# Keys' side of a last attention layer loaded ahead into dead rows, and its fill reordered

## The chip, the cores and the metric

One NeuronCore of a Trainium2 chip runs the whole kernel. Its engines are TensorE (PE, with its weight load PEld), VectorE (DVE), ScalarE (ACT), GpSimd (POOL) and SyncE (SP), which here does nothing but wait and issue DMAs. Each engine runs its own instructions in order and waits on semaphores. The metric is the time of one execution on the device in microseconds.

## The reference, cut to what matters

The rows `x` are 8 sequences of 256 rows of 256 features, and the context `ctx` has the same shape. Two layers follow each other:

```
layer 0: x = LN(x)                                      # pre-norm, then
         y = LN(y + mha(y, y))     ; y = LN(y + mha(y, ctx))   # 16 heads of 16, masked
         y = LN(y + relu(y@w1)@w2)
         x = x + tanh(g0) * y
         x = x + tanh(g0f) * moe_top2(LN(x))            # 8 experts, 256 -> 1024 -> 256
layer 1: q = rope(LN(x) @ Wq) ; k = rope(ctx @ Wk) ; v = ctx @ Wv
         x = x + tanh(g1) * (softmax(q k^T / 8) v @ Wo) # no context depends on x
         x = x + tanh(g1f) * moe_top1(LN(x))
```

Keys and values of layer 1 come from the context alone, queries from the rows that layer 0 leaves.

## The kernel before, in words

The program is three stages with a barrier between them, all matrices in f32, scores in split bf16 parts.

**Attention stage** (`attention_pipeline`). 16 units (8 sequences x 2 attentions) move through a pipeline of beats, one unit per beat, 16 heads per beat; `b` is the beat. In the beat `b`, head 14, TensorE turns the context of unit `b + 4` (`turn_context`, units 8 to 15 only) into a PSUM bank, and ScalarE copies it to the one SBUF tile `cT` (`bring_context`); keys and values of that unit are projected from `cT` in the next beat. SP's program is written out per beat: `stack(b + 2)`, `spread_parts(b + 3, 0)`, `spread_parts(b + 3, 1)`, `max_to_queries(b + 1)`, loads. Two PSUM banks are shared by all small tasks in turn, in the order of `TASKS`.

**Expert stage** (`feed_forward_and_experts`). First 8 sequences pass a dense feed-forward; VectorE forms the new rows (`rows`, `new_rows`), the router picks two experts (`top_experts`, `destinations`), and POOL scatters the normed rows `Y` to DRAM by expert (`scatter`). Then `SLOTS` = 39 slots of 128 rows run, 12 of them (`EARLY_SLOTS`) before all sequences are sorted. Per slot: SP loads its rows from DRAM (`load`, 128 KB, into the one tile `xs`), TensorE turns them (`turn_slot`), VectorE copies the expert's first matrix to one of two places (`expert_matrix`, line 2644), TensorE multiplies up (`up_slot`, line 2350), ScalarE applies relu, TensorE multiplies down (`down_slot`, line 2362), VectorE adds the bias (`slot_rows`), SP stores (`store`). TensorE's order in the loop is up s, turn s + 1, down s - 1. SP's is `load(s + 1)`, `store(s - 1)`. After the last scatter nothing reads `Y` any more.

**Last stage** (`rotary_and_experts`). SP loads weights, tables and contexts (`load_rotary`) into the space where the experts' matrices come later. A fill precedes the beats: for sequences 0 to 2, POOL gathers each row's two expert outputs with indirect DMAs (`gather`, four calls, line 1624), VectorE adds them to `X` (`sum_rows`, line 1847) and takes moments (`input_moments`), POOL computes the inverse roots in 14 tiny steps (`input_roots`, lines 134 to 141), VectorE norms (`input_norm`, line 151, into `Y`), TensorE turns (`turn_rows`) and projects queries (line 1185); the contexts are turned (`turn_context`, line 1176), copied to `cT`, and projected to keys (line 1185) and values (line 1208). VectorE rotates keys and queries (`turned`, lines 1771 and 1773). Each is then split into three bf16 parts by POOL and ScalarE in turn (`parts`: lines 1600, 1605, 1610 on POOL, with two copies on ScalarE between; `split` on ScalarE), and SP writes them to DRAM and reads them back as stacks (`spread_parts`, `stack`). Scores, their maxima, and the beats follow. In a beat `b`, head 14, `turn_context(b + 4)` and `bring_context(b + 4)` run here too. `first_expert` is POOL's load of expert 0 over the space of the contexts.

The order of POOL's work in the fill is written out by hand:

```python
gather(0); gather(1); input_roots(0); parts(0, 1); parts(0, 0); input_roots(1)
gather(2); parts(1, 1); parts(1, 0); input_roots(2); gather(3); parts(2, 1); gather(4); parts(2, 0)
```

Of the kernel before, what the change touches and what calls it, by code (L numbers as in the profile page):

```python
# [14 lines left out]
P = 128  # L15
# [322 lines left out]
def attention_pipeline(nc, tag, c, mem, X, Y, cross, masks, fills, keys_out, loads, ff):  # L338
# [7 lines left out]
    with ExitStack() as ctx:  # L346
# [47 lines left out]
        filled0 = sem("filled0")  # L394
# [9 lines left out]
        def _(sp):  # L404
# [40 lines left out]
            sp.wait_ge(filled0, 16 * (len(fills) + 1))  # L445

# [155 lines left out]
        def _(act):  # L602
# [264 lines left out]
FILL = ("c", 0), ("k", 0), ("v", 0), ("x", 0), ("q", 0), ("c", 1), ("k", 1), ("v", 1), ("x", 1), ("q", 1), ("c", 2), ("k", 2), ("v", 2)  # L867
LAST_FILL = {2: (("x", 2),), 5: (("q", 2),), 9: (("m", 0),), 12: (("x", 3),), 14: (("c", 3),)}


def rotary_tasks(b, h):
# [4 lines left out]
    units = [(k, QUADS * b + d if k == "o" else b + d) for k, d in TASKS.get(h, ()) + ROUTE_TASKS.get(h, ())]  # L876
# [15 lines left out]
def rotary_memory(nc, ctx, tag, w_in, keys, key_off, tables, ctx_in, stack_rows):  # L892
# [11 lines left out]
    w = {"wq": by_chunk(part("W2", 1, 0)), "wk": by_chunk(part("W2", 1, 1)), "wv": by_chunk(part("W2", 1, 2)), "wo": sb("wo", [P, NC, D])}  # L904
# [3 lines left out]
    return {"w": w, "w_in": w_in, "keys": keys, "key_off": key_off, "tables_in": tables, "ctx_in": ctx_in, "stack_rows": stack_rows,  # L908
            "W1": W1, "W2": W2, "w1s": w1s,
            "C": [by_chunk(part(("W1", "W2")[m // 4], 0, m % 4)) for m in range(B)],  # L910
            "tables": {k: by_chunk(part("W1", 1, i)) for i, k in enumerate(tables)},
            "fq": part("W2", 1, 3), "fk": part("W1", 2, 0), "rq": part("W1", 2, 1), "rk": part("W1", 2, 2), "tq": part("W1", 2, 3),
            "tk": part("W2", 2, 0), "cT": by_chunk(part("W2", 2, 1)),
# [13 lines left out]
def load_context_of(sp, mem, n):  # L927

    sp.dma_start(mem["C"][n], mem["ctx_in"][n].rearrange("(u p) d -> p u d", p=P)).then_inc(mem["c_in"][n], 16)


def load_rotary(sp, mem):

    w, w_in = mem["w"], mem["w_in"]

    def matrix(k, done):
        sp.dma_start(w[k][:, :, :], w_in[k].rearrange("(c p) n -> p c n", p=P)).then_inc(done, 16)
# [10 lines left out]
    load_context_of(sp, mem, 0)  # L948
    matrix("wk", mem["k_in"])
    columns("bk", mem["k_in"])  # L950
    table("cosk", mem["k_in"])
    table("sink", mem["k_in"])
    matrix("wv", mem["v_in"])
    row("bv", mem["v_in"])
    sp.dma_start(mem["mcu"][:, :], mem["keys"].rearrange("b (u p) -> p (b u)", p=P), allow_slow_non_contiguous=True).then_inc(mem["v_in"], 16)
    matrix("wq", mem["q_in"])
# [3 lines left out]
    load_context_of(sp, mem, 1)  # L960
    load_context_of(sp, mem, 2)
# [13 lines left out]
def rotary_and_experts(nc, tag, c, mem, X, Y, L, gate, yd, dest, weight, gate_f, ids_dram, rows_dram, out, w1_in, w2_in, b1_in, b2_in, wg_in, bg_in):  # L975
# [3 lines left out]
    W1, W2, w1s = mem["W1"], mem["W2"], mem["w1s"]  # L979
# [7 lines left out]
    with ExitStack() as ctx:  # L987
# [5 lines left out]
        xT, cT, aT, yT = sb("xT", [P, NC, SEQ]), mem["cT"], sb("aT", [P, NC, SEQ]), sb("yT", [P, NC, SEQ])  # L993
# [163 lines left out]
        def _(pe):  # L1157
            ident, identb = c["ident"], c["identb"]

            def turn_rows(m):  # L1160
# [3 lines left out]
                for cc in range(NC):  # L1164
                    for u in range(NU):
                        ins = nc.tensor.transpose(dst[:, cc * SEQ + u * P:cc * SEQ + (u + 1) * P],
                                                  here(Y, m)[:, u, cc * P:(cc + 1) * P], ident[:, :])
                ins.then_inc(filled("x", m), 1)

            def turn_context(m):  # L1170
                pe.wait_ge(mem["c_in"][m], 16)
                pe.wait_ge(*free("c", m))
                dst = bank_of("c", m)
                for cc in range(NC):
                    for u in range(NU):
                        ins = nc.tensor.transpose(dst[:, cc * SEQ + u * P:cc * SEQ + (u + 1) * P],
                                                  C[m][:, u, cc * P:(cc + 1) * P], ident[:, :])
                ins.then_inc(filled("c", m), 1)
# [10 lines left out]
            def queries(m):  # L1189
                if m == 0:  # L1190
                    pe.wait_ge(mem["q_in"], 16 * 4)
# [3 lines left out]
            def keys(m):  # L1195
                if m == 0:
                    pe.wait_ge(mem["k_in"], 16 * 4)
                pe.wait_ge(*taken("c", m))
                product("k", m, w["wk"], cT)

            def project_values(m):
                if m == 0:
                    pe.wait_ge(mem["v_in"], 16 * 3)
                pe.wait_ge(*free("v", m))
                dst = bank_of("v", m)
                for u in range(NU):
                    for kc in range(NC):
                        ins = nc.tensor.matmul(dst[:, u * D:(u + 1) * D], cT[:, kc, u * P:(u + 1) * P], w["wv"][:, kc, :],  # L1208
# [144 lines left out]

            turn_context(0)
            keys(0)
            project_values(0)
            turn_rows(0)
            queries(0)
            turn_context(1)
            keys(1)  # L1360
            project_values(1)
            turn_rows(1)
            queries(1)
            turn_context(2)
# [4 lines left out]
            for h in range(H):  # L1369
# [9 lines left out]
                if h == 14:  # L1379
                    turn_context(3)  # L1380
            early = lambda n: 0 <= n < EARLY_ONES - 1
            for b in range(0, M):
                for h in range(H):
# [18 lines left out]
                    if h == 14 and has(b + 4):  # L1402
                        turn_context(b + 4)
# [48 lines left out]
        def _(act):  # L1452
# [5 lines left out]

            def bring_context(m):
                if m >= 1:  # L1460
                    act.wait_ge(*full("v", m - 1))
                act.wait_ge(*full("c", m))
                nc.scalar.activation(flat(cT[:, :, :]), bank_of("c", m)[:, :], ACT.Copy).then_inc(emptied("c", m), 1)
# [68 lines left out]
            bring_context(0)  # L1532
            bring_rows(0)
            split(0, 1)
            bring_context(1)
            split(0, 0)
            bring_rows(1)
            split(1, 1)
            bring_context(2)
# [5 lines left out]
            bring_context(3)  # L1545
            early = lambda n: 0 <= n < EARLY_ONES - 1
            for b in range(0, M):
                for h in range(H):
# [14 lines left out]
                    if h == 14 and has(b + 4):  # L1563
                        bring_context(b + 4)
# [31 lines left out]
        def _(pool):  # L1596
# [71 lines left out]
            def first_expert():  # L1668
                pool.wait_ge(*full("c", M - 1))
# [91 lines left out]
        def _(dve):  # L1761
# [92 lines left out]
            def input_norm(n):  # L1854
                dve.wait_ge(rooted0, n + 1)
                normal_rows(nc, here(X, n), here(Y, n), t0).then_inc(x_normed, 1)
# [118 lines left out]
            dve.wait_ge(mem["v_in"], 16 * 3)  # L1975
            nc.vector.tensor_copy(mcf[:, :], mem["mcu"][:, :]).then_inc(kept_in, 1)
            value_rows(0)
            sum_rows(1)
            input_moments(1)
            dve.wait_ge(mem["q_in"], 16 * 4)  # L1980
            queries(0)
            turned_keys(1)
            input_norm(1)
            value_rows(1)
# [170 lines left out]

def feed_forward_memory(nc, ctx, a):
# [646 lines left out]
```

## Time and profile before

| what | value |
|---|---|
| median of 3 runs | 1408.83 us (1404.21 to 1412.75) |
| profiled execution, its own time | 1403.39 us |
| span of its instructions | 1401.5 us |
| TensorE busy | 1219.7 us (87%), mean granted clock 0.945 |
| VectorE busy | 769.8 us (55%) |
| ScalarE busy | 560.6 us (40%) |
| POOL busy | 500.7 us (36%) |
| DMA, mean over the span | 111 GB/s |
| expert stage, first slot to last | 583.8 to 896.8 us |
| last stage, fill | 900.7 to about 1000.1 us |

The span runs from the first to the last instruction of the core; the execution's own time is 1.9 us more. Busy shares are averages over stages with different limits, so a stage has to be read by itself. The granted clock is the share of TensorE's full clock (2.4 GHz) that it was given; 0.50 is 1.2 GHz.

### The profile page before, as it was taken

How to read it: one execution, taken by the hardware profiler on the slowest of the kernel's cores; microseconds unless marked ns; L12 is line 12 of the kernel's file. 1: busy time of each engine (PE TensorE's matmuls, PEld its weight loads, DVE VectorE, ACT ScalarE, POOL GpSimd, SP SyncE). 2: the span in 40 equal slices, each digit the busy share in tenths (PEclk: the TensorE clock that was granted, in tenths of full speed). 3: DMA queues.
4: the chain of work that ended last, by engine and by line, in shares of the span. 5: the costliest groups of instructions: out<-in, count | busy, mean ns of one | idle time of the engine just before them, and what ended most of it. 6: DMA issues, size and time to landing. Idle time of an engine off the chain costs nothing. (4 is left out here: it accounts for less than half of the span.)

```text
span 1401.5 us, 27155 instructions
## 1 busy us (share of the span) xinstructions
PE 1219.7 (87%) x8465; PEld 973.2 (69%) x8520; DVE 769.8 (55%) x2825; ACT 560.6 (40%) x1350; POOL 500.7 (36%) x895
## 2 busy tenths in 40 slices
PE   4699999999998999898999999656687878689996
PEld 3466667777755888788888898533455655589995
DVE  4687777777783487842412121147788876533331
ACT  2265565666665332233333333111354546133331
POOL 3334354454524244420000000256765543433331
PEclk9799999999999999999999999865799999799999
DMA  4776785756520950111111111356364597511110
GB/s 118 163 169 189 198 205 156 162 155 152 145 63 11 356 195 31 42 58 35 36 34 36 34 38 32 85 131 149 99 146 105 85 279 230 180 33 43 41 34 6
DMA packets 126580, 156.16 MB, mean 111 GB/s; under 512 B 19531, under 2 KB 112089, under 8 KB 121564
## 3 DMA queue, kind: packets, MB, share of 16 engines
q1 hardware_dynamic: 116648, 127.14, 35.2%
q0 software_dynamic: 9792, 27.30, 6.3%
q8 instruction: 71, 1.16, 0.4%
q14 instruction: 69, 0.57, 0.2%
HBM read 104.43 MB, written 52.32 MB: 112 GB/s over the span
## 5 line engine op out<-in xcount | busy, mean ns | idle before, releaser
L764 DVE CUSTOM_DVE_ANT_0 att_masked_scores<-att_S,Bm 128x256 bf16<-128x256 f32 x512 | 192.5, 419 | 69.4 <-PE att_S L508 55.4
L645 ACT ACTIVATE att_PT<-att_T 128x512 f32<-128x512 f32 x256 | 151.4, 595 | 93.6 <-PE att_T L527 84.8
L2437 ACT ACTIVATE moe_hT<-moe_H,moe_b 128x128 f32<-128x128 f32 x312 | 89.0, 369 | 194.9 <-PE moe_H L2350 193.6
L2350 PE MATMUL moe_H<-moe_aT,ff_w 128*128 128x128 f32 x1248 | 146.2, 275 | 8.4 <-DVE ff_w L2644 8.4
L2350 PEld LDWEIGHTS moe_H<-moe_aT,ff_w 128*128 128x128 f32 x1248 | 145.1, 192 | 11.7 <-DVE ff_w L2644 9.9
L2362 PE MATMUL moe_Z<-moe_W,moe_hT 128*128 x624 | 142.5, 381 | 0.8 <-DVE moe_z L2651 0.8
L1624 POOL DMA_INDIRECT L_W<-yd,dest x32 | 31.3, 977 | 278.4 <-POOLq L52 269.9
L2362 PEld LDWEIGHTS moe_Z<-moe_W,moe_hT 128*128 128x128 f32 x624 | 115.4, 190 | 15.5 <-issue 1.2
L2651 DVE TENSOR_TENSOR moe_z<-moe_Z,moe_b 128x256 f32<-128x256 f32 x39 | 16.5, 424 | 199.5 <-PE moe_Z L2362 199.5
L508 PE MATMUL att_S<-L_KS,L_QS 96*128 96x256 bf16 x512 | 99.3, 276 | 19.6 <-DMA L_KS<-att_k_dram 14.5
L527 PE MATMUL att_T<-L_QS,L_KS 99*128 99x256 bf16 x512 | 98.7, 273 | 4.8 <-issue 2.3
L1800 DVE TENSOR_REDUCE out_mx<-out_S 128x2 f32<-128x512 f32 x128 | 85.7, 683 | 17.1 <-PE out_S L1218 14.8
L1520 ACT ACTIVATE X<-out_T,L_b 128x128 f32<-128x128 f32 x184 | 52.5, 370 | 98.4 <-PE out_T L1337 97.1
L1337 PEld LDWEIGHTS out_T<-out_xT,L_w1s 128*128 128x128 f32 x736 | 87.5, 196 | 4.7 <-issue 2.1
L1337 PE MATMUL out_T<-out_xT,L_w1s 128*128 128x128 f32 x736 | 88.2, 279 | 2.9 <-issue 1.5
L1486 ACT ACTIVATE L_W<-out_T 128x512 f32<-128x512 f32 x128 | 72.7, 596 | 39.7 <-PE out_T L1236 37.2
L1350 PE MATMUL out_S<-L_W,X 128*128 x368 | 83.5, 380 | 2.1 <-DVE out_ys L1962 2.1
L527 PEld LDWEIGHTS att_T<-L_QS,L_KS 99*128 99x128 bf16 x512 | 50.6, 99 | 38.9 <-issue 1.1
L525 PE MATMUL att_T<-BmT,identb 128*128 128x512 bf16 x201 | 77.0, 383 | 0.4
L1218 PE MATMUL out_S<-L_W 97*128 97x256 bf16 x256 | 54.7, 303 | 25.9 <-DVE out_mx L1800 20.3
L1350 PEld LDWEIGHTS out_S<-L_W,X 128*128 128x128 f32 x368 | 68.1, 190 | 11.5 <-issue 3.2
L508 PEld LDWEIGHTS att_S<-L_KS,L_QS 96*128 96x128 bf16 x512 | 48.0, 98 | 33.6 <-DMA L_KS<-att_k_dram 16.0
(465 smaller groups left out, 2385.5 us busy)
## 6 DMA issues: line engine op xcount, KB each, us to landing
moe_W<-in_L_ffn_W SPq DMA_DIRECT2D x16, 1024.0 KB, 13.7
xd<-zero SPq DMA_DIRECT2D x12, 1280.0 KB
L_W<-in_L_ffn_W POOLq DMA_DIRECT2D x12, 1024.0 KB, 15.3
att_q_dram<-att_pq SPq DMA_DIRECT2D x16, 384.0 KB
att_k_dram<-att_pk SPq DMA_DIRECT2D x16, 384.0 KB
L_QS<-att_q_dram SPq DMA_DIRECT2D x16, 384.0 KB
L_KS<-att_k_dram SPq DMA_DIRECT2D x16, 384.0 KB
moe_xs<-xd SPq DMA_DIRECT2D x39, 128.0 KB
```

The lines of the kernel that those rows point to most:

```text
L508: ins = nc.tensor.matmul(bankS[h % 2][:, u * SEQ:(u + 1) * SEQ], QS[0:ROWS, m % 3, h, u * P:(u + 1) * P], KS[0:ROWS, m % 3, h, :], start=T ...
L525: nc.tensor.matmul(dst[:, :], identb[:, :], masks[m // B][1][:, :], start=True, stop=False)
L527: ins = nc.tensor.matmul(dst[:, u * SEQ:(u + 1) * SEQ], KS[0:ROWS_ALL, m % 3, h, u * P:(u + 1) * P], QS[0:ROWS_ALL, m % 3, h, :], start=Fa ...
L645: nc.scalar.activation(PT[:, h % 8, :], bankT[h % 2][:, :], ACT.Exp).then_inc(exp_done, 1)
L764: ins = nc.vector.tensor_tensor_reduce(masked_scores[:, h % 2, u, :], bankS[h % 2][:, u * SEQ:(u + 1) * SEQ], masks[m // B][0][:, u * SEQ: ...
L1337: ins = nc.tensor.matmul(bankH[half][:, f * P:(f + 1) * P], matrix[:, cc, k * P:(k + 1) * P], xT[:, s % 2, cc * P:(cc + 1) * P], start=(cc ...
L1350: ins = nc.tensor.matmul(bankY[:, 0:D], eT[:, s % 2, f * P:(f + 1) * P], matrix[:, f, :], start=(f == 0), stop=(f == NF - 1))
L1486: nc.scalar.activation(PT[h % 8], bankT[h % 2][:, :], ACT.Exp).then_inc(exp_done, 1)
L1800: nc.vector.tensor_reduce(mx[:, m % 2, :, h:h + 1], bankS[h % 2][:, :].rearrange("p (u k) -> p u k", u=NU), AXX, ALU.max).then_inc(max_don ...
L2350: ins = nc.tensor.matmul(bankH[half][:, f * P:(f + 1) * P], w1s[:, cc, g * P:(g + 1) * P], xT[:, s % 2, cc * P:(cc + 1) * P], start=(cc == ...
L2362: ins = nc.tensor.matmul(bankZ[:, 0:D], eT[:, s % 2, f * P:(f + 1) * P], w2e[:, f, :], start=(f == 0), stop=(f == NF - 1))
L2437: ins = nc.scalar.activation(eT[:, s % 2, g * P:(g + 1) * P], bankH[half][:, f * P:(f + 1) * P], ACT.Relu, bias=b1[:, bass.ds(e * NF + g, 1)])
```

## The change

**Attention stage.** After ScalarE has filled `cT` for units 8 to 15, SP stores it to a DRAM tensor `turned_ctx` (`keep_context`), once per unit, before the spreads of the same beat. ScalarE's `bring_context` waits for the store of the unit before.

**Expert stage.** `turn_router(6)` and its copy on ScalarE move from ahead of slot 0 to behind it, `logits(6)` and `rank(6)` one slot later, `expert_matrix(0)` ahead of `new_rows(6)`, `expert_matrix(2)` ahead of `new_rows(7)`, `top_experts(6)` and `destinations(6)` one slot later. At slot 12, ahead of the load of slot 13's rows, SP issues eight loads (`load_entry`) into `Y`: `wk`, `wv`, `wq`, the two tables of the keys, and the turned contexts 0 to 2.

**Last stage.** No context is turned: keys and values multiply from the loaded turned contexts, the five others come from `turned_ctx` through `load_rest`. `cT` and the `c` tasks of the shared banks are gone. `input_norm` writes to two tiles `xn` in turn instead of `Y`. `load_rotary` keeps only the biases, the mask, the two tables of the queries and the constant rows. The orders of all engines in the fill are written anew. `first_expert` waits for the values of sequence 7 where it waited for its turned context.

```diff
+            def keep_context(m):
+                sp.wait_ge(*taken("c", m))
+                sp.dma_start(turned_ctx[m - B], flat(cT[:, :, :])).then_inc(ctx_kept, 16)
             for b in BEATS:
                 if has(b + 2):
                     stack(b + 2)
+                if has(b + 3) and cross(b + 3):
+                    keep_context(b + 3)
...
                 act.wait_ge(*full("c", m))
+                if m > B:
+                    act.wait_ge(ctx_kept, 16 * (m - B))
...
+ENTRY_CONTEXTS = 3
+ENTRY = "wk", "wv", "wq", "cosk", "sink"
+def load_entry(sp, Y, entry, entered):
+    contexts, places = entry_places(Y)
+    for k in ENTRY:
+        sp.dma_start(places[k], entry[k].rearrange("(c p) n -> p c n", p=P)).then_inc(entered, 16)
+    for n in range(ENTRY_CONTEXTS):
+        sp.dma_start(contexts[n], entry["contexts"][n].rearrange("p (c t) -> p c t", c=NC)).then_inc(entered, 16)
...
+                if s == EARLY_SLOTS:
+                    sp.wait_ge(r_turned, B)
+                    load_entry(sp, Y, entry, entered)
                 if s + 1 < SLOTS:
                     load(s + 1)
                 if s >= 1:
                     store(s - 1)
...
+                if n == B - 1:
+                    expert_matrix(0)
                 new_rows(n - 1)
...
-            expert_matrix(0)
             rows(B - 1)
+            expert_matrix(1)
             for s in range(SLOTS):
...
+                if s == 0:
+                    expert_matrix(2)
+                    new_rows(B - 1)
+                if s >= 2 and s + 1 < SLOTS:
                     expert_matrix(s + 1)
...
             gather(0)
+            parts(0, 1)
+            input_roots(0)
             gather(1)
-            input_roots(0)
-            parts(0, 1)
             parts(0, 0)
             input_roots(1)
+            parts(1, 1)
             gather(2)
-            parts(1, 1)
             parts(1, 0)
             input_roots(2)
...
             nc.vector.memset(V[:, :, :, :], 1.0).then_inc(ready0, 1)
+            dve.wait_ge(mem["k_in"], 16)
+            turned_keys(0)
+            dve.wait_ge(mem["v_in"], 16 * 2)
+            nc.vector.tensor_copy(mcf[:, :], mem["mcu"][:, :]).then_inc(kept_in, 1)
+            value_rows(0)
             sum_rows(0)
             input_moments(0)
-            dve.wait_ge(mem["k_in"], 16 * 4)
-            turned_keys(0)
+            turned_keys(1)
+            value_rows(1)
             input_norm(0)
```

On ScalarE the fill begins `split(0, 1)`, `bring_rows(0)`, `split(0, 0)`, `first_part(1, 1)`, `bring_rows(1)`, `second_part(1, 1)`; on TensorE keys and values of sequences 0 and 1, then their rows and queries, then keys and values of sequence 2.

## Rows read from the trace of the kernel before

**Rows 1.** Windows of the fill and of a later beat; columns stand in the head line.

```profile
core 0: us, PE busy (x) PEld busy (x) DVE busy (x) ACT busy (x) POOL busy (x), PEclk, DMA share, GB/s
900.70:1000.10 99.40, 57.10 (x190) 36.60 (x190) 53.68 (x147) 13.68 (x23) 66.02 (x127) 0.63 0.63 150
...
1040.00:1050.00 10.00, 9.17 (x80) 5.65 (x78) 8.54 (x23) 4.55 (x10) 7.12 (x18) 1.00 0.80 185
```

**Rows 2.** What POOL waited for, 898 to 1004 us: us in total, times, longest.

```profile
POOL out_xve L134 <- DVE out_xmv L118: 8.3, 2, 4.5
POOL L_W L1605 <- ACT L_W L1476: 7.3, 7, 2.9
...
POOL L_W L1600 <- DVE L_W L1773: 2.0, 1, 2.0
```

**Rows 3.** Timeline of POOL in the fill: start, us, then line, operation, idle before.

```profile
900.75 0.99 POOL L1624 DMA_INDIRECT L_W<-yd,dest  x1 [269.85 <-POOLq L52]
902.04 0.97 POOL L1624 DMA_INDIRECT L_W<-yd,dest  x1 [0.30 <-issue]
...
914.37 0.21 POOL L134 TENSOR_SCALAR out_xve<-out_xmv 128x2 f32<-128x2 f32 x1 [3.86 <-DVE out_xmv L118]
...
918.14 1.26 POOL L1600 TENSOR_TENSOR L_W<-L_W 128x512 f32<-128x512 f32 x1
...
941.29 1.28 POOL L1600 TENSOR_TENSOR L_W<-L_W 128x512 f32<-128x512 f32 x1
...
946.31 1.26 POOL L1600 TENSOR_TENSOR L_W<-L_W 128x512 f32<-128x512 f32 x1
```

**Rows 4.** Timeline of VectorE (DVE) in the fill.

```profile
911.34 1.88 DVE L1847 SCALAR_TENSOR_TENSOR X<-L_W,weight,X 128x256 f32<-128x256 f32 x4 [8.44 <-DMA L_W<-yd,dest]
...
918.22 1.65 DVE L151 TENSOR_SCALAR Y<-X,out_xmv,out_xr 128x256 f32<-128x256 f32 x2 [2.39 <-POOL out_xr L141]
...
926.82 0.48 DVE L1773 SCALAR_TENSOR_TENSOR L_W<-out_A,L_bq,L_W 128x256 f32<-128x256 f32 x1
...
1000.28 1.65 DVE L151 TENSOR_SCALAR Y<-X,out_xmv,out_xr 128x256 f32<-128x256 f32 x2 [3.89 <-POOL out_xr L141]
```

**Rows 5.** Timeline of TensorE (PE), last stage.

```profile
921.78 3.75 PE L1185 MATMUL out_A<-out_xT,L_W 128*128 128x256 f32 x8 [0.73 <-ACT out_xT L1457]
...
1016.67 0.60 PE L1176 MATMUL out_B<-ident,L_W 128*128 128x128 f32 x4
```

**Rows 6.** Timeline of TensorE, slots of the expert stage.

```profile
583.77 3.84 PE L2350 MATMUL moe_H<-moe_aT,ff_w 128*128 128x128 f32 x32 [2.43 <-DVE ff_w L2644]
...
590.51 3.84 PE L2350 MATMUL moe_H<-moe_aT,ff_w 128*128 128x128 f32 x32 [1.89 <-DVE ff_w L2644]
...
599.09 3.84 PE L2350 MATMUL moe_H<-moe_aT,ff_w 128*128 128x128 f32 x32 [0.86 <-DVE ff_w L2644]
...
685.48 0.44 PE L2337 MATMUL moe_T<-ident,moe_xs 128*128 128x128 f32 x2 [0.18 <-DMA moe_xs<-xd]
...
690.26 3.84 PE L2350 MATMUL moe_H<-moe_aT,ff_w 128*128 128x128 f32 x32 [0.85 <-DVE ff_w L2644]
```

**Rows 7.** Timeline of SP's DMA issues, slots and fill.

```profile
682.32 0.33 SPq L2237 DMA_DIRECT2D yd<-moe_z  x1
683.40 0.34 SPq L2233 DMA_DIRECT2D moe_xs<-xd  x1
...
974.50 2.64 SPq L929 DMA_DIRECT2D L_W<-in_ctx  x5
```

**Rows 8.** Context loads of the last stage, from issue to landing.

```profile
DMA to landing us min/median/max: 2.9/6.1/7.2
```

**Rows 9.** Windows of 2 us in the fill, columns as in rows 1.

```profile
978.00:980.00 2.00, 1.60 (x6) 0.39 (x6) 2.00 (x6) 0.62 (x1) 1.21 (x2) 0.50 0.95 184
982.00:984.00 2.00, 0.00 (x0) 0.00 (x0) 0.21 (x1) 0.00 (x0) 1.50 (x9) 0.50 1.11 349
1002.00:1004.00 2.00, 1.34 (x8) 0.63 (x12) 2.00 (x5) 1.70 (x5) 1.16 (x1) 0.60 0.00 0
1004.00:1006.00 2.00, 2.00 (x20) 0.80 (x13) 2.00 (x5) 0.88 (x3) 1.90 (x2) 0.54 0.00 0
```

More of the change, by code:

```diff
@@ L889, in rotary_banks, with rotary_memory @@
     return {task: (i % 2, i // 2) for i, task in enumerate(order)}
-def rotary_memory(nc, ctx, tag, w_in, keys, key_off, tables, ctx_in, stack_rows):
+def rotary_memory(nc, ctx, tag, w_in, keys, key_off, tables, turned_ctx, stack_rows, Y):
     sb = lambda n, s, d=F32: ctx.enter_context(nc.sbuf_tensor(f"{tag}_{n}", s, d))
@@ L903, in rotary_memory @@
     PARTS = 3 * NC * SEQ // 2
-    w = {"wq": by_chunk(part("W2", 1, 0)), "wk": by_chunk(part("W2", 1, 1)), "wv": by_chunk(part("W2", 1, 2)), "wo": sb("wo", [P, NC, D])}
+    contexts, entered = entry_places(Y)
+    w = {"wo": sb("wo", [P, NC, D]), **{k: entered[k] for k in ("wq", "wk", "wv")}}
     w.update({k: sb(k, [P, NC]) for k in ("bq", "bk")})
@@ L907, in rotary_memory @@
     stacks = lambda a: a.rearrange("p (e h t) -> p e h t", e=3, h=H)
-    return {"w": w, "w_in": w_in, "keys": keys, "key_off": key_off, "tables_in": tables, "ctx_in": ctx_in, "stack_rows": stack_rows,
+    return {"w": w, "w_in": w_in, "keys": keys, "key_off": key_off, "tables_in": tables, "ctx_in": turned_ctx, "stack_rows": stack_rows,
             "W1": W1, "W2": W2, "w1s": w1s,
-            "C": [by_chunk(part(("W1", "W2")[m // 4], 0, m % 4)) for m in range(B)],
-            "tables": {k: by_chunk(part("W1", 1, i)) for i, k in enumerate(tables)},
+            "C": contexts + [by_chunk(part(("W1", "W2")[m // 4], 0, m % 4)) for m in range(ENTRY_CONTEXTS, B)],
+            "tables": {"cosk": entered["cosk"], "sink": entered["sink"], **{k: by_chunk(part("W1", 1, i)) for i, k in enumerate(tables)}},
+            "xn": [by_chunk(part("W2", 1, i)) for i in range(2)],
             "fq": part("W2", 1, 3), "fk": part("W1", 2, 0), "rq": part("W1", 2, 1), "rk": part("W1", 2, 2), "tq": part("W1", 2, 3),
-            "tk": part("W2", 2, 0), "cT": by_chunk(part("W2", 2, 1)),
+            "tk": part("W2", 2, 0),
             "pq": three(half["W2", 2][:, 2 * NC * SEQ:2 * NC * SEQ + PARTS]), "pk": three(half["W2", 3][:, 0:PARTS]),
@@ L968, in load_rest @@
     w, w_in = mem["w"], mem["w_in"]
-    for n in range(3, B):
+    for n in range(ENTRY_CONTEXTS, B):
         load_context_of(sp, mem, n)
@@ L1166, in turn_rows @@
                         ins = nc.tensor.transpose(dst[:, cc * SEQ + u * P:cc * SEQ + (u + 1) * P],
-                                                  here(Y, m)[:, u, cc * P:(cc + 1) * P], ident[:, :])
+                                                  xn[m % 2][:, u, cc * P:(cc + 1) * P], ident[:, :])
                 ins.then_inc(filled("x", m), 1)
[L1170 to L1178, printed above, removed]
             def product(kind, m, wt, src):
@@ L1352, in down_slot @@
                 ins.then_inc(y_ready, 1)
[L1354 to L1364, printed above, removed]
+            for m in range(2):
+                keys(m)
+                project_values(m)
+            for m in range(2):
+                turn_rows(m)
+                queries(m)
             keys(2)
@@ L1530, in split @@
                 second_part(m, side)
-            bring_context(0)
+            split(0, 1)
             bring_rows(0)
-            split(0, 1)
-            bring_context(1)
             split(0, 0)
+            first_part(1, 1)
             bring_rows(1)
-            split(1, 1)
-            bring_context(2)
+            second_part(1, 1)
             split(1, 0)
@@ L1668, in first_expert @@
             def first_expert():
-                pool.wait_ge(*full("c", M - 1))
+                pool.wait_ge(*full("v", M - 1))
                 load_expert(pool, 0)
@@ L1855, in input_norm @@
                 dve.wait_ge(rooted0, n + 1)
-                normal_rows(nc, here(X, n), here(Y, n), t0).then_inc(x_normed, 1)
+                if n >= 2:
+                    dve.wait_ge(*full("x", n - 2))
+                normal_rows(nc, here(X, n), xn[n % 2], t0).then_inc(x_normed, 1)
                 dve.wait_ge(x_normed, n + 1)
@@ L2385, in _ @@
                 if s == 0:
+                    turn_router(B - 2)
+                if s == 1:
                     logits(B - 2)
-                if s == 1:
+                if s == 2:
                     rank(B - 2)
-                if s == 2:
                     turn_router(B - 1)
@@ L2719, in weights_of @@
                     "gain": a[f"L0_xattn_{norm}_g"], "shift": a[f"L0_xattn_{norm}_b"]}
+        wkv, bkv = a["L1_xattn_Wkv"], a["L1_xattn_bkv"]
+        w = {**{k: a["c_L1_" + k] for k in ("wq", "bq", "wk", "bk")}, "wv": wkv[:, D:2 * D], "bv": bkv[D:2 * D],
+             "wo": a["L1_xattn_Wo"], "bo": a["L1_xattn_bo"]}
         with ExitStack() as f:
```

93 lines of the change are left out of this document (32 added, 61 removed).

## The prediction

> **What bounds the kernel now.** I read the windows first, since the change touches four places with different limits. In the expert stage (about 580 to 900 us) TensorE is the bound. The fill of the last stage, 900.7 to 1000.1 us, is the weak stretch: TensorE is busy 57.1 of 99.4 us at a mean clock of 0.63, POOL 66.0 us, and no engine is full, while a later beat has TensorE 9.17 and VectorE 8.54 of 10 us at full clock [rows 1]. Of POOL's gaps there some are waits for others: 8.3 us in two waits for moments, 2.0 us for VectorE's turned keys, and one wait of 2.9 us for ScalarE where 0.74 is usual, in all 8.3 + 2.0 + 2.1 = 12.4 us [rows 2]. The timelines show POOL paces the rest: it runs roots, gathers and parts back to back, and VectorE waits 3.89 us for the roots of the fifth sequence at the fill's end [rows 3, 4]. So the fill is worth at most these 12.4 us to a reordering that leaves POOL's work as it is.
>
> **Attention stage: contexts kept.** Added: eight stores of 256 KB, one a beat, issued on SP between `stack(b + 2)` and the spreads, and a wait on ScalarE before `bring_context` for the store of one beat earlier. `cT` was filled a beat before SP asks, so SP does not wait; the store lands in microseconds [rows 8] and the beat is over 20 us. Behind it in SP's order stand the two spreads, which wait for parts of their own. Cost 0; were that cover gone, one 256 KB transfer (at most 2.9 us, rows 8) would delay one stack.
>
> **Expert stage, turn from rows to slots.** `expert_matrix(0)` moves ahead of `new_rows(6)`, and `turn_router(6)` behind the first slot. Before, TensorE waited 2.43, 1.89 and 0.86 us for the copies of slots 0, 1 and 2 [rows 6]. Slot 0 now starts some 2.6 us sooner, but copy 1 still stands behind the same VectorE work (`new_rows(6)`, `destinations(5)`, `rows(7)`; only the copy changed places), so up-projection 1 still starts at 590.5: the first gain turns into a longer wait there. Copy 2 now precedes `new_rows(7)`, so 0.86 us is gained. Against it, the two short waits have become one of about 4.3 us. After a wait of that size the clock fell: in 1002 to 1006 us it was 0.60 and 0.54, which is 2 x 0.40 + 2 x 0.46 = 1.7 us of full-clock work lost [rows 9]. I take the loss: -0.9 + 1.7 = **+0.8** (bounds -0.9 and +0.8).
>
> **Expert stage, entry load.** Eight DMAs of 256 KB (three weights, two tables, three contexts, 2.10 MB) enter SP's queue at slot 12, ahead of the load of slot 13's rows. SP is free there after the store at 682.3, and issued load 13 at 683.4; TensorE turned it at 685.48 after waiting 0.18 us for that very DMA [rows 6, 7]. So this load has no slack. Each issue takes SP about 0.52 us (five contexts in 2.64, rows 7), eight take 4.1. If only the issue counts, load 13 leaves at 687.5 and lands at 689.4, 3.9 us late; TensorE waited 0.85 us soon after for the copy behind `pack_destinations` [rows 6], which is absorbed: **+3.1**, the lower bound. If the bytes also go first, with the rows themselves they are 2.23 MB. The best rate in a stretch of context loads is 349 GB/s, the worst 184 [rows 9]; a lone 256 KB needs 2.9 us, of which 0.75 is bytes at 349, so 2.1 is fixed [rows 8]. Landing is then 682.7 + 2.1 + 6.4 = 691.2, 5.7 us late, 4.8 after the absorbed wait; TensorE stands idle nearly 6 us, and I add 2.5 us for the clock, between one fall (1.7) and two (3.4). **+7.3**. At 184 GB/s: 682.7 + 2.1 + 12.1 = 696.9, 10.5 net, with 3.4 for the clock **+13.9**, the upper bound. I take 7.3, since these are contiguous rows as in the faster stretch, while the slow one held small-row stacks.
>
> The trace has large loads and small ones behind them landing late. The Trainium skill ("DMA: Bandwidth & Descriptors", Queues, rings and completion order) says that on each DMA engine descriptors are consumed in ring order. By that rule the 128 KB load waits for all 2.10 MB; without it, the sum would take the lower bound. The same page (Specifications) gives about 358 GB/s from HBM; by that figure, an estimate, the bytes take 6.2 us and the sum changes by 0.2.
>
> **Last stage, fill.** Removed: turning three contexts in the fill (four with the last half), their copies, 2 MB of loads at the entry. POOL's pieces keep their lengths: a gather 4 x 1.27 - 0.3 = 4.8, roots 3.8 (914.37 to 918.14), parts 5.05 (941.29 to 946.31) [rows 3]. New order, from POOL's first at 900.75:
> gather(0) to 905.6. Keys(0) need no load but the bias: TensorE 3.75 at half clock [rows 5], VectorE 1.6, ready at about 905.6. Parts(0,1) to 910.7. Gather(0) lands 2.9 later, 908.5 (before, at 911.3 behind the loads, rows 4); sums 1.9 and moments 1.0: 911.4, a wait of **0.7**. Roots(0) to 915.3, gather(1) to 920.1. Parts(0,0) needs queries(0), which before came 9.1 us after the start of the norm (918.22 to 927.30, rows 4), so 924.4: a wait of **4.3**. Then roots(1), parts(1,1) (second part behind `bring_rows(1)`: **0.2**), gather(2), parts(1,0), roots(2), whose moments wait for gather(2) (**0.8**), gather(3), parts(2,1), gather(4), parts(2,0), whose queries wait behind ScalarE's `split(2, 1)` (**0.8**); the rest as before. Waits 6.8 in place of 12.4: **-5.6**. Bounds: if gather(0) lands as late as before, 2.8 less, -2.8; if TensorE is at full clock for queries(0) and the turns, 2.0 us of that wait go, -7.6. What is late next is the roots of sequence 4, still POOL's. The copy of `mcu` is now ahead of the first sums; its DMA is issued third and has until 908.5.
>
> **Last stage, beats.** Five turns of a context leave TensorE (0.60 us each, rows 5) with their ScalarE copies: 3.0 us at most. VectorE is nearly as full as TensorE in a beat [rows 1], so most is hidden: **-1.0** (0 to -3.0). `first_expert` waits for v(7) instead of c(7), which POOL's own `keep_values(7)` has awaited already: 0.
>
> **Sum.** 0 + 0.8 + 7.3 - 5.6 - 1.0 = +1.5 on the profiled execution's own 1403.39 (span 1401.5 and 1.9 around it): 1404.9. The median of the runs is 1408.83, 5.4 above that execution, so **1410.3**. A step of 0.5% is 7 us, about what this kernel's measurement can tell from nothing.
>
> **Rivals.**
> *Only the issue costs.* Slot 13's rows overtake the entry load; the entry load costs 3.1. For it: no row shows this pair of transfers; against: load 13 is the last in the same queue. 0.8 + 3.1 - 5.6 - 1.0 = -2.7: 1406.1.
> *The fill gives more.* TensorE stays warm between the early keys and queries(0), no clock is lost at the slots, and the beats gain all five turns: -0.9 + 3.1 - 7.6 - 3.0 = -8.4, 1400.4. For it: keys and values of two sequences now run in one piece; against: some 4 us of idle follow them, and the clock's mean of 0.63 in the fill [rows 1].
> *Slower: the entry load at the slow rate.* One stall at slot 13 worth 13.9 (above): 0.8 + 13.9 - 5.6 - 1.0 = +8.1, 1416.9. It decides for slower from a stall of 12.8. For it: the stretch at 184 GB/s also held context loads [rows 9]; against: its small rows.
>
> **Chances.** Forecast 0.48 (of it 0.02 below and 0.04 above the 0.5% lines), issue only 0.12, more from the fill 0.22, slow load 0.18, with what resembles it. Faster 0.22 + 0.02 = 0.24, same 0.42 + 0.12 = 0.54, slower 0.18 + 0.04 = 0.22. The two outer cases are 1400.4 and 1416.9; with the runs' own scatter the range is 1400 to 1418. The forecast's own range is 1405 to 1415.
>
> **What would show it.** Right: one TensorE gap of 5 to 7 us before the turn of slot 13, released by the rows' DMA, with half clock behind it; up-projection 1 still released by its copy; POOL's first parts at 905.6 after the stage's start, its wait before parts(0,0) near 4 us, and the roots of sequence 4 some 6 us nearer the stage's start. Wrong: slot 13 on time, a stage start that moved for other reasons, a POOL wait for queries(0) over 8 us, or scores that wait for a stack in the beats.

## The result, and the profile after

The changed kernel takes 1414.61 us (median of 20 runs, 1408.08 to 1421.87), the kernel before 1403.97 (20 runs, 1397.66 to 1412.75). The ratio is 1.0071, 95% interval 1.0058 to 1.0085: slower by 0.7%, some 10 us. The forecast was +1.5 us. It was made on a median of 1408.83 us from three runs, which twenty runs put at 1403.97; so the changed kernel's time lies in the forecast's range (1405 to 1415) by luck: the time before was taken 4.9 us too high, and that hid half of the miss. The difference, which is what matters, is missed by 9 us, and a slowdown above 0.5% had a chance of only 0.22. The profiled execution of the changed kernel has a span of 1414.1 us, against 1401.5.

I cut both spans at the same instructions: the first turn of slot 0, the turns of slots 12 and 14 on TensorE, POOL's first gather in the last stage (gather(0)) and its gather(5) at the end of the fill. The lengths, in us:

| kernel | to slot 0 | slots 0 to 12 | slots 12 to 14 | slot 14 to gather(0) | fill, to gather(5) | rest | span |
|---|---|---|---|---|---|---|---|
| before | 581.0 | 96.8 | 16.1 | 206.8 | 90.1 | 410.6 | 1401.5 |
| changed | 584.4 | 98.2 | 25.4 | 206.0 | 92.0 | 408.1 | 1414.1 |

The largest item is at slots 12 to 14, **+9.2** (25.37 against 16.13). It is one stall and the half clock behind it (0.50 from 694 to 702 us). TensorE's timeline of the changed kernel in the slots, with the two slots of the turn from rows to slots first:

```profile
585.54 3.81 PE L2341 MATMUL moe_H<-moe_aT,ff_w 128*128 128x128 f32 x32 [0.72 <-issue]
...
593.51 5.44 PE L2341 MATMUL moe_H<-moe_aT,ff_w 128*128 128x128 f32 x32 [3.50 <-ACT moe_aT L2420]
...
603.35 3.73 PE L2341 MATMUL moe_H<-moe_aT,ff_w 128*128 128x128 f32 x32
...
697.44 0.69 PE L2328 MATMUL moe_T<-ident,moe_xs 128*128 128x128 f32 x2 [7.35 <-DMA moe_xs<-xd]
697.93 6.26 PE L2353 MATMUL moe_Z<-moe_W,moe_hT 128*128 x16
704.02 3.73 PE L2341 MATMUL moe_H<-moe_aT,ff_w 128*128 128x128 f32 x32
```

Where 0.18 us of waiting stood before the turn of slot 13 [rows 6], 7.35 stand now, and the down-projection behind it lasts 6.26 us where 3.62 to 3.65 is usual. SP's issues of the changed kernel, and its window over the stall:

```profile
687.12 0.33 SPq L2224 DMA_DIRECT2D yd<-moe_z  x1
687.50 0.43 SPq L2137 DMA_DIRECT2D Y<-in_c_L_wk  x1
...
690.05 1.42 SPq L2139 DMA_DIRECT2D Y<-turned_ctx  x3
692.21 0.35 SPq L2220 DMA_DIRECT2D moe_xs<-xd  x1
```

```profile
core 0: us, PE busy (x) PEld busy (x) DVE busy (x) ACT busy (x) POOL busy (x), PEclk, DMA share, GB/s
...
690.00:700.00 10.00, 2.65 (x8) 2.17 (x8) 3.82 (x12) 1.52 (x5) 0.00 (x0) 0.65 0.57 188
```

The rows' load leaves at 692.21 and is awaited until 697.4, 5.2 us, and the granted clock of the window is 0.65.

The fill was to become 5.6 us shorter and is **1.9 longer**. The window of the whole fill, to the norm of sequence 4 [rows 1], and what POOL waited for in it [rows 2]:

```profile
913.95:1015.40 101.45, 51.00 (x174) 31.46 (x173) 56.11 (x148) 11.51 (x19) 66.27 (x128) 0.61 0.53 127
```

```profile
POOL out_xve L134 <- DVE out_xmv L118: 10.3, 2, 6.7
...
POOL L_W L1575 <- ACT L_W L1451: 4.7, 6, 1.0
POOL L_W L1565 <- DVE L_W L1738: 3.8, 2, 3.4
```

POOL is busy as before (66.0, now 66.3). TensorE has 6 us less to do, which buys nothing. The waits of my sum were 12.4 us before, I forecast 6.8, and they are 10.3 + 3.8 + 0.3 = 14.4 (the 0.3 is what the longest wait for ScalarE, 1.0, has above the usual 0.74). POOL's timeline and VectorE's show where [rows 3, 4]:

```profile
913.98 0.98 POOL L1589 DMA_INDIRECT L_W<-yd,dest  x1 [278.75 <-POOLq L52]
...
917.79 0.95 POOL L1589 DMA_INDIRECT L_W<-yd,dest  x1 [0.30 <-issue]
919.14 1.26 POOL L1565 TENSOR_TENSOR L_W<-L_W 128x512 f32<-128x512 f32 x1 [0.41 <-DVE L_W L1738]
...
930.87 0.21 POOL L134 TENSOR_SCALAR out_xve<-out_xmv 128x2 f32<-128x2 f32 x1 [6.68 <-DVE out_xmv L118]
...
942.99 1.43 POOL L1565 TENSOR_TENSOR L_W<-L_W 128x512 f32<-128x512 f32 x1 [3.36 <-DVE L_W L1738]
```

```profile
927.85 1.87 DVE L1812 SCALAR_TENSOR_TENSOR X<-L_W,weight,X 128x256 f32<-128x256 f32 x4 [6.75 <-DMA L_W<-yd,dest]
...
942.82 3.77 DVE L1812 SCALAR_TENSOR_TENSOR X<-L_W,weight,X 128x256 f32<-128x256 f32 x4
...
967.99 1.87 DVE L1812 SCALAR_TENSOR_TENSOR X<-L_W,weight,X 128x256 f32<-128x256 f32 x4 [3.95 <-DMA L_W<-yd,dest]
```

Keys and first parts are there when forecast (919.14 is 5.2 us behind the stage's start). But gather(0), whose last issue ended at 918.7, is summed only at 927.85, 9.1 us later, and not 2.9. The view of the DMA queues over two of these microseconds, 922 to 924, shows what was under way:

```profile
GB/s 0 0 0 0 0 0 0 0 0 0 0 0 0 0 0 0 0 0 0 492 0 0 492 0 0 0 0 0 0 0 0 492 0 0 0 0 0 0 0 0
DMA packets 7, 0.07 MB, mean 37 GB/s; under 512 B 4, under 2 KB 4, under 8 KB 4
...
q1 hardware_dynamic: 6, 0.07, 27.0%
q0 software_dynamic: 1, 0.00, 0.0%
```

Here q0 carries the gathers and q1 what SP issues. Three packets of these two microseconds carry nearly all of the bytes: 492 GB/s in a slice of 0.05 us is 24.6 KB each. That is one row of the constants for the stacks, which are 3 partitions of 24 KB, issued twice on SP. In the kernel before they were issued at 911.27 us, when gather(0) had landed; in the changed kernel they are issued while its last call is under way:

```profile
918.07 0.68 SPq L963 DMA_DIRECT2D L_W<-in_c_stack_rows  x2
```

From 924 to 928 us nine more packets of q0 follow, the last of the gather. Between the last 24 KB packet and these stands more than a microsecond without any packet on record (924 to 925.1), and they come beside the store of the key parts, which SP issued at 924.22. So the profile shows the company, and not what the last packets waited for; the experiments below have to tell.

### The profile page after: what moved, and what is told of

Its sections match the earlier page's. It is cut to its first block and busy times, and to the rows that moved or that the text cites. A ratio compares the mean times of both kernels' runs of the same rounds, so it can differ in the third digit from the quotient of the medians.

```text
span 1414.1 us, 27133 instructions
## 1 busy us (share of the span) xinstructions
PE 1224.7 (87%) x8488; PEld 973.4 (69%) x8488; DVE 773.2 (55%) x2825; ACT 554.8 (39%) x1342; POOL 500.2 (35%) x895
## 5 line engine op out<-in xcount | busy, mean ns | idle before, releaser
L2429 ACT ACTIVATE moe_hT<-moe_H,moe_b 128x128 f32<-128x128 f32 x312 | 88.7, 368 | 197.3 <-PE moe_H L2341 196.0
L2341 PEld LDWEIGHTS moe_H<-moe_aT,ff_w 128*128 128x128 f32 x1248 | 148.3, 195 | 9.3 <-DVE ff_w L2637 6.5
L2644 DVE TENSOR_TENSOR moe_z<-moe_Z,moe_b 128x256 f32<-128x256 f32 x39 | 16.5, 424 | 206.5 <-PE moe_Z L2353 206.5
L515 PE MATMUL att_S<-L_KS,L_QS 96*128 96x256 bf16 x512 | 99.2, 275 | 25.3 <-DMA L_KS<-att_k_dram 18.9
L532 PE MATMUL att_T<-BmT,identb 128*128 128x512 bf16 x256 | 98.5, 385 | 0.5 <-ACT att_PT L654 0.2
L1490 ACT ACTIVATE X<-out_T,L_b 128x128 f32<-128x128 f32 x184 | 52.3, 368 | 97.9 <-PE out_T L1322 97.5
```

The source lines that it names most:

```text
L515: ins = nc.tensor.matmul(bankS[h % 2][:, u * SEQ:(u + 1) * SEQ], QS[0:ROWS, m % 3, h, u * P:(u + 1) * P], KS[0:ROWS, m % 3, h, :], start=T ...
L532: nc.tensor.matmul(dst[:, :], identb[:, :], masks[m // B][1][:, :], start=True, stop=False)
L2341: ins = nc.tensor.matmul(bankH[half][:, f * P:(f + 1) * P], w1s[:, cc, g * P:(g + 1) * P], xT[:, s % 2, cc * P:(cc + 1) * P], start=(cc == ...
L2429: ins = nc.scalar.activation(eT[:, s % 2, g * P:(g + 1) * P], bankH[half][:, f * P:(f + 1) * P], ACT.Relu, bias=b1[:, bass.ds(e * NF + g, 1)])
```

## The experiments

All were timed in five rounds beside the kernel before; ratios are to it, with 95% intervals. The changed kernel's is 1.0071 (1.0058 to 1.0085), from its own rounds. The table cuts one profile of each as above, in us.

| kernel | ratio | to slot 0 | slots 0 to 12 | 12 to 14 | 14 to gather(0) | fill | rest |
|---|---|---|---|---|---|---|---|
| entry_behind | 1.0006 (0.9989 to 1.0024) | 583.5 | 98.1 | 17.1 | 206.2 | 91.5 | 407.8 |
| entry_spread | 1.0061 (1.0037 to 1.0085) | 584.1 | 97.1 | 16.8 | 211.9 | 92.9 | 408.0 |
| entry_near | 1.0014 (0.9991 to 1.0037) | 583.1 | 96.8 | 16.1 | 206.2 | 92.1 | 408.5 |
| rows_late | 1.0055 (1.0034 to 1.0075) | 580.7 | 95.5 | 23.4 | 205.6 | 89.0 | 408.1 |
| gathers_first | 1.0071 (1.0051 to 1.0090) | 582.9 | 98.2 | 23.4 | 205.6 | 93.8 | 408.5 |
| behind_rows | 0.9986 (0.9969 to 1.0003) | 582.1 | 97.5 | 16.7 | 206.2 | 89.8 | 407.4 |
| kept_alone | 0.9998 (0.9978 to 1.0017) | 582.7 | 97.3 | 16.1 | 206.7 | 90.1 | 409.3 |
| slots_alone | 0.9994 (0.9976 to 1.0013) | 586.0 | 96.1 | 16.1 | 206.6 | 89.7 | 410.3 |
| gather_sooner | 0.9980 (0.9959 to 1.0002) | 585.1 | 97.6 | 16.8 | 205.5 | 90.2 | 409.4 |
| small_late | 0.9950 (0.9928 to 0.9972) | 579.1 | 98.5 | 16.8 | 206.4 | 87.2 | 409.9 |
| both_fill | 0.9970 (0.9949 to 0.9992) | 585.4 | 96.9 | 16.5 | 206.3 | 88.7 | 409.7 |
| keys_sooner | 0.9956 (0.9934 to 0.9977) | 582.1 | 99.2 | 16.4 | 206.6 | 84.4 | 408.8 |

**entry_behind: the entry load behind the rows of slot 13.**

```diff
+                if s + 1 < SLOTS:
+                    load(s + 1)
                 if s == EARLY_SLOTS:
                     sp.wait_ge(r_turned, B)
                     load_entry(sp, Y, entry, entered)
-                if s + 1 < SLOTS:
-                    load(s + 1)
```

> The changed kernel, but the load of slot 13's rows is issued ahead of the eight entry loads. Theory A (the 9.0 us that the changed kernel loses at slot 13 come from the rows' load standing behind 2.1 MB in one queue): the turn of slot 13 starts on time; the load of slot 14's rows leaves some 6 us later and has a whole slot of 7.9 us, so it costs at most 1 to 2 us. The kernel is 7 to 9 us faster than the changed one, so within 2 us of the kernel before plus what attention and fill have added: ratio to the kernel before 1.001 +- 0.002. Theory B (the transfers compete with any load of rows, whatever the order in the queue): the stall only moves to slot 14, ratio stays at 1.006 to 1.008.

Theory A holds. Slots 12 to 14 take 17.1 us in place of 25.4, and the ratio's interval leaves out theory B's 1.006. TensorE's timeline:

```profile
689.36 0.44 PE L2328 MATMUL moe_T<-ident,moe_xs 128*128 128x128 f32 x2 [0.20 <-DMA moe_xs<-xd]
...
698.77 0.44 PE L2328 MATMUL moe_T<-ident,moe_xs 128*128 128x128 f32 x2 [0.81 <-DMA moe_xs<-xd]
```

**entry_spread and entry_near: one entry load per slot.** The second differs from the first only in the place within the slot. The first came out as its theory B had it, which left open whether the bytes cost wherever they are issued.

```diff
 # entry_spread, slots 12 to 19: load(s + 1), store(s - 1), then
+                if 0 <= s - EARLY_SLOTS < ENTRY_CONTEXTS + len(ENTRY):
+                    load_entry(sp, Y, entry, entered, s - EARLY_SLOTS)
 # entry_near: the same two lines between load(s + 1) and store(s - 1)
```

> The changed kernel, but one entry load per slot, slots 12 to 19, each behind the load and the store of that slot. Theory A: no slot waits for its rows, since 256 KB land in about 3 us of a slot of 7.9 us; the whole 9.0 us come back, ratio to the kernel before 1.000 to 1.001. Theory B: each of eight loads of rows lands about 0.7 us late (256 KB at 349 GB/s); since the rows' load has only some tenths of slack, up to 8 x 0.7 = 5.6 us stay, ratio about 1.004 to 1.005.

> The changed kernel, but one entry load per slot, slots 12 to 19, straight behind that slot's load of rows and ahead of its store. In the version with each entry load behind the store it left 1.3 us ahead of the next rows' load and slots 13 to 20 lasted 8.4 to 9.0 us in place of 7.7. Theory A2 (only what stands ahead of a rows' load in the queue delays it): here each entry load has 6 us until the next rows' load, no slot is longer, ratio to the kernel before 0.9990 to 1.0015, like the version with all eight behind the rows of slot 13. Theory B2 (any 256 KB beside a slot's traffic costs some 0.7 us, wherever it is issued): ratio 1.005 to 1.006 again.

Theory B holds for entry_spread: 1.0061, with 1.004 to 1.005 inside the interval and 1.001 outside. Spread out, the same bytes still cost most of what they cost in one piece: 211.9 us from slot 14 to the last stage in place of 206.2. SP's issues, and the turn that waits:

```profile
703.00 0.44 SPq L2138 DMA_DIRECT2D Y<-in_L_xattn_Wkv  x1
704.30 0.34 SPq L2222 DMA_DIRECT2D moe_xs<-xd  x1
```

```profile
706.56 0.44 PE L2331 MATMUL moe_T<-ident,moe_xs 128*128 128x128 f32 x2 [0.95 <-DMA moe_xs<-xd]
```

SP sits in the store's wait until just before the next rows' load is due, so an entry load written behind the store leaves 1.3 us ahead of those rows, eight times. Written ahead of the store, behind the rows' load, it costs nothing that can be seen (206.2; theory A2, and B2's 1.005 is outside the interval). So it is what was issued ahead of the rows that delays them, and not the bytes as such. All of these loads went through SP's queue; whether loads issued at the same moment through another engine's queue would delay the rows as much was not tried.

**rows_late and gathers_first: what holds gather(0) back.**

```diff
 # rows_late: the loads of the constant rows leave load_rotary
             for m in range(2):
                 spread_parts(m, 1)
+                if m == 0:
+                    sp.wait_ge(gathered[0], 16 * NU * TOP)
+                    load_constant_rows(sp, mem)
                 stack(m, 1)
 # gathers_first, on POOL
             gather(0)
+            gather(1)
             parts(0, 1)
             input_roots(0)
-            gather(1)
```

> The changed kernel, but the two loads of constant rows for the stacks (3 partitions x 24 KB each) are issued only when gather(0) has landed. In the changed kernel the last of gather(0)'s packets come 9.1 us after its issue, at 922 to 926 us, while a handful of 24 KB packets occupy single DMA engines. Theory C (those long packets hold the gather's last ones): gather(0) lands by 4 us after its issue, POOL's wait for moments falls from 6.7 to 1 to 2 us, queries(0) come 5 us sooner and the kernel is 3 to 5 us faster than the changed one: ratio to the kernel before 1.004. Theory D (another cause, POOL's own work behind the gather or the tiny elements of mask and bias): the landing and the wait of 6.7 us stay, ratio stays 1.007.

> The changed kernel, but POOL issues gather(1) right behind gather(0), as before the change, and then parts(0,1) and the roots. Theory D (POOL's arithmetic straight behind the gather holds its last packets back): gather(0) lands some 5 us sooner, queries(0) come 5 us sooner, 3 to 5 us faster than the changed kernel, ratio 1.004. Theory C (the constant rows hold them): gather(0) still lands 9 us after its issue; POOL only spends its wait on gather(1), the chain of sums, roots, norm, turn and queries of sequence 0 stays where it was, so POOL waits longer ahead of parts(0,0); within 1 us of the changed kernel, ratio 1.006 to 1.008.

Theory C in kind, at a good half of its size. With the constant rows late, gather(0) is summed 5.4 us after its last issue (910.0 to 915.38), where theory C had 4, and POOL waits 3.3 us for the moments in place of 6.7; the fill is 3.0 us shorter than the changed kernel's. The time alone does not tell the theories apart: the interval of 1.0055 takes in C's 1.004 and D's 1.007. The profiles do, since they repeat: from the last issue to the sums gather(0) took 9.1, 8.8, 8.6 and 9.6 us in the four profiles with the constant rows beside it and POOL's order of the changed kernel (changed, entry_behind, entry_near, entry_spread), and 5.4, 3.8 and 3.7 in the three with only the constant rows late (rows_late, behind_rows, gather_sooner). With gather(1) first, gather(0) still takes 10.6 us (914.8 to 925.44), and the wait only moves in front of parts(0,0); the ratio's interval leaves out theory D's 1.004. VectorE of rows_late, POOL of gathers_first:

```profile
915.38 1.86 DVE L1819 SCALAR_TENSOR_TENSOR X<-L_W,weight,X 128x256 f32<-128x256 f32 x4 [3.17 <-DMA L_W<-yd,dest]
```

```profile
940.57 1.43 POOL L1565 TENSOR_TENSOR L_W<-L_W 128x512 f32<-128x512 f32 x1 [8.28 <-DVE L_W L1738]
```

**behind_rows: entry_behind and rows_late together.**

> The changed kernel with both changes that helped alone: the entry load behind the rows of slot 13, and the constant rows behind the landing of gather(0). If the two places are independent the gains add: 0.65% and 0.25% off the changed kernel's 1.007, so 0.998 to the kernel before (0.996 to 1.000). If POOL or VectorE is the limit of the fill whatever lands, the second gain is not seen here: 1.0005.

The gains add: 0.9986 where the sum had 0.998, with 1.0005 outside the interval, and the profile has both (16.7 and 89.8). SP's issues and the longest wait of its next stack show how slow the constant rows are:

```profile
913.11 0.92 SPq L967 DMA_DIRECT2D L_W<-in_c_stack_rows  x2
921.33 1.24 SPq L1074 DMA_DIRECT2D L_W<-out_k_dram  x3
```

```profile
SPq L1074 <- DMA L_W<-in_c_stack_rows: 5.6, 1, 5.6
```

That is 7.3 us from the end of the issue for 144 KB. The store of the key parts (384 KB) had been issued 0.4 us ahead of them, so part of the 7.3 us can be its.

**kept_alone and slots_alone: two parts of the change put alone on the kernel before** (`keep_context` with ScalarE's wait; the new order of copies, router turn and sorting).

> The kernel before, with only the contexts' stores of the attention stage added (keep_context on SP and ScalarE's wait), nothing reads them. Theory E (nothing in the attention stage waits for them; the 4.3 us by which the changed kernel's profile is late at 577 us arise in beats of unchanged code and are scatter of single executions): ratio 1.000 +- 0.001. Theory F (the store ahead of the spreads delays a stack in the first beats, where the traffic is high, and costs the 2 to 4 us of the profile): ratio 1.0015 to 1.003.

> The kernel before, with only the turn from rows to slots reordered (copies of the matrices of slots 0 and 2 earlier, turn_router(6) behind slot 0, the tasks of sequence 6 one slot later). My forecast was +0.8 us: ratio 1.0005. From the profile of the changed kernel, relative to its last ranking, slot 0 starts 2.6 us sooner, slot 1 1.35 us sooner but at half clock, and slots 2 and 3 at the old time: 0.0 to 0.4 us, ratio 1.0000 to 1.0003. Rival: the first gain is kept somewhere, -0.9 us or more: 0.9994 or less.

Theory E for the first: no difference, with theory F's range outside the interval but for its lowest end (1.0015, 1.0017). The second is 0.9994 with 1.0 well inside: neither my +0.8 nor the rival's gain can be told from nothing. Its attention stage is that of the kernel before, and it reaches slot 0 at 586.0 where the kernel before did at 581.0. The time to slot 0 is 579.1 to 585.4 us in the eleven profiles whose instructions up to there are the changed kernel's. So it scatters over single executions by more than the changed kernel's +3.4, which says nothing.

**gather_sooner, small_late, both_fill, keys_sooner: how much the fill still holds.** All start from behind_rows; keys_sooner from small_late.

```diff
 # small_late: after load_rotary (bk and bv only), ahead of the first spread
+            sp.wait_ge(gathered[0], 16 * NU * TOP)
+            load_queries_side(sp, mem)      # bq, cosq, sinq, mcu
 # gather_sooner, on POOL
             input_roots(1)
+            gather(2)
             parts(1, 1)
-            gather(2)
 # keys_sooner, on POOL and likewise on ScalarE
             gather(1)
+            parts(1, 1)
             parts(0, 0)
             input_roots(1)
-            parts(1, 1)
```

> The version with the entry load behind the rows of slot 13 and the constant rows behind gather(0) (ratio 0.9986), and in POOL's fill gather(2) ahead of parts(1,1), as before the change. In that version gather(2) lands 6.6 us after its last issue and POOL waits 4.6 us for the moments that hang on it, since only parts(1,0), 5.1 us, lie between. Theory G (the wait is the gather's landing): with 10 us of parts between, the wait of 4.6 us disappears and the roots come 4 to 5 us sooner: 0.3% less, ratio 0.9955 (0.994 to 0.997). Theory H (POOL then waits elsewhere, for queries(1) or for ScalarE's copies, or the following waits grow): gain under 1 us, ratio 0.998 to 0.999.

> The version with the entry load behind the rows of slot 13 and the constant rows behind gather(0) (ratio 0.9986), and the queries' bias and tables and the mask (2,048 elements of one byte) too are issued only when gather(0) has landed. Theory I (gather(0) still lands 4.9 to 5.4 us after its last issue because of these loads): it lands about 3 us after, POOL's wait for the first moments falls from 2.4 to about 0 us, and queries(0) come 2 us sooner: ratio 0.9965 to 0.9975. Theory J (the landing is the gather's own, the loads only fill free engines): 0.9985 or, if the tables now come late for queries(0), above.

> Both edits of the fill together: gather(2) ahead of parts(1,1), and the queries' side and the mask behind the landing of gather(0). If theories G and I hold and add: ratio 0.9940 (0.992 to 0.996). If the second gain only enlarges POOL's wait for queries(0): 0.9955. If neither holds: 0.9985.

> The fastest version so far (entry load behind the rows of slot 13; constant rows, queries' side and mask behind gather(0); ratio 0.995), and parts(1,1) ahead of parts(0,0) on POOL and ScalarE. In that version POOL waits 1.4 us for the first moments, 3.4 us for queries(0) and 3.8 us for the moments behind gather(2), 8.6 us in all. Theory K (POOL's own work fills the wait for queries(0), and with parts(1,1) gone from between, gather(2) has some 9 us to land): the waits of 3.4 and 3.8 us go, one of 2 to 4 us for queries(1) comes: 3 to 5 us less, ratio 0.992 (0.990 to 0.994). Theory L (waits only change places, as when gather(2) was moved ahead of parts(1,1): the chain sums, roots, norm, turn, queries, roots of the next sequence is as long as POOL's work): within 1 us, ratio 0.9945 to 0.9955.

gather_sooner: theory H. POOL's wait for the moments of sequence 2 falls from 4.6 to 1.8 us, but one of 3.0 us for queries(1) comes, the one that parts(1,1) had covered, and the fill stays at 90.2 (behind_rows: 89.8). small_late: theory I, and more than it had. gather(0) has landed when SP, which waits for it, issues `bq` at 907.45, 1.8 us after its last issue (1.8 also in both_fill and keys_sooner, where the same loads are late; theory I had 3), the fill is 2.6 us shorter than that of behind_rows, and the whole interval of the ratio is below 1. both_fill gives 0.9970, where 0.9940 was the sum: the two do not add, and in the same rounds it is 3.6 us slower than small_late. VectorE of small_late, which no longer waits for the gather, and SP:

```profile
907.87 3.66 DVE L1825 SCALAR_TENSOR_TENSOR X<-L_W,weight,X 128x256 f32<-128x256 f32 x4
```

```profile
907.45 0.38 SPq L963 DMA_DIRECT2D L_bq<-in_c_L_bq  x1
```

keys_sooner: in the profile the fill is 2.8 us shorter than small_late's (84.4), with these waits left on POOL:

```profile
POOL L_W L1577 <- DVE L_W L1750: 3.4, 2, 3.1
POOL out_xve L134 <- DVE out_xmv L118: 3.3, 2, 1.8
```

That is 6.7 us of waits in place of 8.6, a smaller cut than theory K had. The times show no gain over small_late: 0.9956, with all of theory L's range inside the interval and of K's only the upper end (0.9934 to 0.994). The shorter fill of one profile speaks for K, the timing for L; that the kernel is faster than small_late is not shown.

## Why the difference was missed by 9 us, point by point

**Attention stage, 0:** right as far as can be told; kept_alone is 0.9998 (0.9978 to 1.0017). The bound beside it misread rows 8, where 2.9 us is the shortest landing and not the longest; nothing hung on it.

**Turn from rows to slots, +0.8:** too small to measure (slots_alone 0.9994). The mechanism was there: slot 0 started 2.6 us sooner relative to the last ranking, then one wait of 3.5 us stood ahead of up-projection 1, and it lasted 5.44 us where 3.84 is usual [rows 6], with a granted clock of 0.50 from 595 to 597 us. It started 1.4 us sooner than before, and not at the same time. As its releaser the profile names ScalarE's copy of the turned rows for the matmuls and the matrix copy for their weight load; the two ended within 0.1 us of each other. From slot 2 on both kernels stand at the same distance from the last ranking.

**Entry load, +7.3:** right in place, cause and nearly in size. Slots 12 to 14 are 9.2, 7.3 and 7.2 us longer in the three profiles with this order (changed, rows_late, gathers_first). The rows' load had no slack, it stood last behind 2.1 MB in its queue, and half clock followed. The stall was the larger part of what was missing: 7.35, 6.38 and 6.58 us in the three profiles, where I had 5.7. The clock was sized rightly: turn and down-projection behind the stall lasted 2.9 us longer, for 2.5 in the sum. "Only the issue costs" (+3.1) is excluded. The Trainium skill ("DMA: Bandwidth & Descriptors", Queues, rings and completion order) has descriptors consumed in ring order on each DMA engine; the stall of 7.35 us, and entry_near against entry_spread, agree.

**Fill, -5.6:** this is the step that failed; it came out at +1.9, 7.5 us off, and outside its bounds. The five waits that I had at 0.7, 4.3, 0.2, 0.8 and 0.8 us measured 6.7, 3.4, 0.3, 3.6 and 0.4, and the roots of sequence 4, which I had 6 us nearer the stage's start, came 1.8 us farther from it (97.5 us, before 95.7). Two of the terms did it. I let gather(0) land "2.9 later", taken from the shortest landing of a context load [rows 8], and took the wait for moments as 0.7; it was 6.7, since the gather took 9.1 us. My bad case was a landing as late as before, 5.8 us after the last issue, when 2 MB of loads stood beside it. With them gone it came 3.3 us later still, because the small loads moved up: the constant rows, formerly issued when gather(0) was landed (911.27, sums at 911.34 [rows 4]), now stood beside it. rows_late takes 3.7 us of the landing away, and small_late, by moving the queries' side and the mask too, brings it down to 1.8. The second term is the 0.8 us for the moments of sequence 2. The new order leaves only parts(1,0), 5.1 us, between gather(2) and the roots that need it; the gather landed 5.7 us after its last issue, sums and moments took 3.0 more, and 5.7 + 3.0 - 5.1 is the wait of 3.6 that I should have priced. The term for queries(0), 4.3, came out at 3.4, since the norm ahead of it took 0.76 us where rows 4 had 1.65.

**Beats, -1.0:** the rest of the span is 407.4 to 409.9 us in the eleven profiles with the changed last stage, and 410.6, 409.3 and 410.3 in the three with the old one: about 1.5 us less in the mean, within the bounds, though the two ranges touch.

Together: 9.2 or 7.2, +1.9 and -1.5 give 8 to 10 us, and the medians differ by 10.6. The time of the slow rival (+8.1) was nearly met, but not by its mechanism: its stall of 13.9 us did not come.

The change is worth having once its loads are placed well: small_late is the changed kernel with three groups of loads issued later (the entry load, the constant rows, the queries' side with the mask), and is 0.5% faster than the kernel before and about 1.2% faster than the changed one (0.9950 against 1.0071).

## What to carry to other kernels

A prefetch into idle bandwidth delays what stands behind it in its queue: issue it right behind the load that has no slack, not in front of it and not behind a wait that ends when the next one is due. When large loads are taken away from a start, look at which small ones now meet the first load that matters, and price its landing by the same kind of transfer in the same company, not by the shortest row. Where several engines pass one chain around, a moved piece of work often uncovers another wait, so list what each piece covered.

## What the runs showed of the hardware that was not expected

- Three-partition loads with rows of 24 KB are slow and hurt others: 144 KB took 7.3 us from the end of their issue to the release of what waits for them (behind_rows, beside a store of 384 KB), single packets of 24 KB were nearly the only traffic for two microseconds (37 GB/s), and the last packets of an indirect gather came only afterwards. Without them the gather landed 5.4, 3.8 and 3.7 us after its issue (rows_late, behind_rows, gather_sooner) in place of 8.6 to 9.6, and with only the two biases (1 and 128 KB) issued ahead of it after 1.8. Whether they share engines with the gather's last packets was not shown separately.
- VectorE's four sums of 256 elements last 1.87 us with POOL idle (changed kernel, 927.85) and 3.66 to 3.77 us beside POOL's arithmetic (small_late, 907.87; changed, 942.82). As an estimate from these rows, sums that start sooner, beside POOL's parts, gave back 1.8 us of what small_late had won.
- The time to the first slot scatters by 6 us over eleven executions with the same instructions up to there (579.1 to 585.4), so the spans of two profiles can't price a part of less than that. The fill scatters less: 91.5 to 92.9 us in four profiles with the same fill.
